# Attention's second tile divided ahead of normalising x, with two steps on the turned x moved back

## The reference

```python
h = _layernorm(x, axis=-1) * (1 + ca) + sa
x = x + ga * _L0_attn_ref(h, W_qkv, b_qkv, W_out, b_out)
h = _layernorm(x, axis=-1) * (1 + cb) + sb
x = x + gb * _L0_ffn_ref(h, w_gate, w_up, w_down)
```

```python
q = elu(q * E ** (-0.5)) + EPS_FEAT
k = elu(k) + EPS_FEAT
# for each token t in order
kv_s = kv_s + einsum('bhe,bhf->bhef', k_t, v_t)
k_s = k_s + k_t
out_t = einsum('bhe,bhef->bhf', q_t, kv_s) / (einsum('bhe,bhe->bh', q_t, k_s) + EPS_DEN)
```

## Time and the profile before

| What | Value |
|---|---|
| Time, median of 3 runs | 2003.87 us (2003.59 to 2005.35) |
| Profiled execution, its own time | 2005.31 us |
| Profiled execution, span of the core | 2003.5 us |
| PE busy | 1961.1 us (98% of the span) |
| DVE busy | 1439.8 us (72%) |
| ACT busy | 906.2 us (45%) |
| POOL busy | 873.5 us (44%) |
| TensorE clock granted, mean | 0.997 of full |

### The profile page before, as it was taken

One profiled execution on the slowest core, in us unless ns is written; L12 is line 12 of the kernel. 1 busy time (PEld: TensorE's weight loads), 2 busy tenths in 40 slices (PEclk: granted clock), 3 DMA queues, 4 the chain that ended last, 5 costly groups with the idle time before them and its releaser, 6 DMA issues. The chain is left out here.

```text
span 2003.5 us, 43850 instructions
## 1 busy us (share of the span) xinstructions
PE 1961.1 (98%) x16008; PEld 1592.4 (79%) x16008; DVE 1439.8 (72%) x2386; ACT 906.2 (45%) x1542; POOL 873.5 (44%) x718
## 2 busy tenths in 40 slices
PE   7999999999999999999899999999999999999999
PEld 4788888888888888887678888888888888888887
DVE  7977887877888877787875857658576585765744
ACT  5444444344444344444254536445364453644533
POOL 2533544444544444443334444444434444344444
PEclk9999999999999999999999999999999999999999
DMA  7223333444433434433475654656546565465553
GB/s 268 66 94 102 112 122 122 127 135 129 121 117 123 133 122 134 130 101 96 158 282 176 209 172 150 226 168 209 175 146 224 169 210 184 144 215 171 169 169 106
DMA packets 202521, 309.81 MB, mean 155 GB/s; under 512 B 16145, under 2 KB 72977, under 8 KB 202386
## 3 DMA queue, kind: packets, MB, share of 16 engines
q1 hardware_dynamic: 201858, 306.78, 48.0%
q10 hardware_dynamic: 528, 1.05, 0.1%
HBM read 225.19 MB, written 82.58 MB: 154 GB/s over the span
## 5 line engine op out<-in xcount | busy, mean ns | idle before, releaser
L1496 POOL TENSOR_TENSOR h_lo<-y_rows,h_hi 128x512 fp32r<-128x512 f32 x192 | 246.6, 1304 | 369.1 <-ACT h_hi L1594 369.0
L461 POOL TENSOR_TENSOR x_res<-y,x_res 128x512 f32<-128x512 f32 x64 | 82.9, 1296 | 293.9 <-DVE y L872 283.4
L851 DVE TENSOR_TENSOR probs<-sc,causal 128x512 f32<-128x512 f32 x256 | 158.3, 680 | 3.9 <-PE sc L1155 2.9
L612 ACT ACTIVATE z_exp<-pj,qk_neg 128x512 f32<-128x512 f32 x128 | 88.0, 687 | 161.5 <-PE pj L1136 159.1
L1136 PE MATMUL pj<-xt_hi,w_hi 128*128 128x512 f32 x512 | 146.3, 407 | 12.0 <-DVE a_t L861 10.8
L1924 PE MATMUL sc<-wd,h_hi 128*128 128x512 f32 x384 | 150.7, 392 | 0.0
L450 POOL TENSOR_TENSOR a_lo<-a_t,a_hi 128x512 fp32r<-128x512 f32 x60 | 82.4, 1373 | 154.5 <-ACT a_hi L626 154.5
L1924 PE MATMUL sc<-wd,h_lo 128*128 128x512 f32 x384 | 149.6, 390 | 0.0
L1136 PE MATMUL pj<-xt_lo,w_hi 128*128 128x512 f32 x512 | 138.8, 393 | 1.7 <-DVE xt_lo L789 1.7
L1136 PE MATMUL pj<-xt_hi,w_lo 128*128 128x512 f32 x512 | 138.2, 392 | 0.0
L1709 DVE TENSOR_TENSOR r_den<-pj,k_tok 128x512 f32<-128x512 f32 x96 | 66.2, 690 | 98.3 <-ACT k_tok L1577 52.6
(11 more groups left out here) (248 smaller groups left out, 5386.5 us busy)
## 6 DMA issues: line engine op xcount, KB each, us to landing
w_hi<-parts SPq DMA_DIRECT2D x48, 1024.0 KB, 5.4
w_lo<-parts SPq DMA_DIRECT2D x48, 1024.0 KB, 5.3
x_mid<-x_res SPq DMA_DIRECT2D x96, 256.0 KB, 2.9
x_res<-in_L_attn_x SPq DMA_DIRECT2D x64, 256.0 KB, 2.8
k_dram<-k_block SPq DMA_DIRECT2D x252, 64.0 KB, 1.8
xg<-in_L_attn_x SPq DMA_DIRECT2D x15, 1024.0 KB, 7.6
x_res<-x_mid SPq DMA_DIRECT2D x60, 256.0 KB, 4.0
full<-x_mid SPq DMA_DIRECT2D x60, 256.0 KB, 3.6
```

The costliest lines, as they stand in the source:

```text
L461: pool.tensor_tensor(out=x_res[:, slot, :], in0=y[:, :], in1=x_res[:, slot, :], op=ALU.add).then_inc(y_ready, 1)
L612: act.activation(z_exp[:, n % 2, :], pj[:, n % 2, :], ACT.Relu, bias=qk_neg[:, 1 - kind, c:c + 1], scale=-scale).then_inc(below_ready, 1)
L851: dve.tensor_tensor(out=probs[:, h, :].rearrange("p (c i) -> p c i", c=C), in0=sc[:, h, :].rearrange("p (c i) -> p c i", c=C), in1=causal[ ...
L1496: pool.tensor_tensor(out=h_lo[b], in0=h[i], in1=h_hi[b].bitcast(F32), op=ALU.subtract).then_inc(h_lo_ready, 1)
```

## The change

Three places, one on each of three engines. No instruction is added or removed.

- DVE, tile 1 of every group but the last: `divide` of tile 1 stands ahead of `norm_x(g + 2)` instead of behind it. Tile 2: `feature(n, other, 7)` stands ahead of `xt_low(g + 2, parity, 0)`.
- ACT: `exp_relu(n, 7)` stands ahead of `xt_full(g + 2, 0)` and `xt_high(g + 2, parity, 0)`.
- PE, tile 2: the first `x_turn` stands behind projection unit 7 (the eighth) instead of between units 6 and 7. Tile 3 is as before.

```diff
@@ scalar, ahead_of_last
             exp_relu(n, 5)
             exp_relu(n, 6)
+            exp_relu(n, 7)
             xt_full(g + 2, 0, x_bank)
             xt_high(g + 2, parity, 0)
-            exp_relu(n, 7)
             if looped:
                 act.wait_ge(down_out, g * 16 + (-16))
             xt_full(g + 2, 1, x_bank)
@@ vector, ahead_of_last
             feature(n, other, 4)
+            divide(g * GT + 1, g, parity, 1)
             norm_x(g + 2)
-            divide(g * GT + 1, g, parity, 1)
 
             mask(g * GT + 2)
...
             feature(n, other, 6)
+            feature(n, other, 7)
             xt_low(g + 2, parity, 0)
-            feature(n, other, 7)
             gate_last(g, 2)
@@ tensor, front
                 project(g + 1, 1 - parity, 3 * t)
-                if t >= 2:
+                if t == 3:
                     wait(pe, probs_ready, (g * GT + t) * HPC + 4)
                     x_turn(g + 2, 2 * t - 4, x_bank)
                 project(g + 1, 1 - parity, 3 * t + 1)
+                if t == 2:
+                    wait(pe, probs_ready, (g * GT + t) * HPC + 4)
+                    x_turn(g + 2, 2 * t - 4, x_bank)
```

## The result

The changed kernel takes 2008.52 us (median of 17 runs, 2006.3 to 2010.92) against 2004.86 (17 runs of the kernel before beside them): a ratio of 1.002, with a 95% interval of 1.0012 to 1.0027. That is 3.7 us more, a small loss of 0.2%. The stall that the change aims at is gone and a little more than its worth has come back elsewhere.

The account below looks back on a forecast made before the run. PE, busy 98% of the span, bounds the kernel. The removed stall is lost again to drawn-out norm_x: 12 groups at 0.2 us plus 3 at 0.1 give +2.7, a median of 2006.6 us; forecast's own range 2002 to 2009.

Parts of the forecast that it names:

- The wait on a_t: PE's projection matmul waiting for DVE's divided attention output: 10.8 us in 15 waits, 15.3 with restarts, all removed.
- The meeting: POOL's a_lo and next operation, pulled forward, meet DVE's third and fourth norm_x; the pair costs 1.92 us of DVE.
- gate_y: DVE, tile 2: ends at 469.83, so scores of tile 3 start later and a group loses 0.2 us.
- the second turn: PE, tile 2: waits 0.9 us for xt_full(0) and starts 0.2 earlier than before, not 1.17.
- The old collision of prod with DVE: POOL's prod against DVE's scan and xt_lo: replaced by feature 6 against prod, feature 6 ending 0.55 us after prod.
- Rival 1: DVE keeps the lock for the third norm_x, only the fourth is drawn out: -10.5 us, 1993.4; chance 0.17.
- Rival 2: No collision that matters, or one with slack behind it: the whole 15.3 us stall goes, 1988.6; chance 0.12.
- rival 3: Scores of tile 3 wait for gate_y in all 15 groups, 0.33 us each: +5.0, 2008.9; chance 0.17.
- a restart at the scores: PE, scores of tile 3: up to 0.14 us paid for resuming; rival 3 takes the full 0.14 in all 15 groups.
- the first turn: PE, tile 2, behind project 7: due at 462.9, said to wait 0.1 to 0.2 us for the masks (462.75).
- the turn costs PE the same at either place: PE, tile 2: moving the first x_turn behind project 7 leaves its cost on PE unchanged.
- The two rules of the Trainium skill: DVE and POOL: the lock rule gives the forecast's sum; the one-SBUF-input rule draws nothing out and gives 1988.6.

Follow-up runs that it names:

- the two runs of the changed order without a meeting: Changed kernel with add_bias and a_lo of each group's second tile cut to 4 columns: 1986.84 us; changed kernel with two norm_x ahead of den_of(n, 0): 1988.36 us.
- one meeting: Changed kernel with add_bias of the second tile of every group cut to 4 columns of 512, a_lo whole: 1992.26 us, ratio 0.9943.
- the control: Kernel before with add_bias and a_lo of the second tile of every group cut to 4 columns of 512: 2002.32 us, ratio 0.9994.

## Why the prediction was right

**What it got right, and the runs that show it.** The wait on a_t was worth about what was worked out: 15.3 us by the rows, 15.5 and 16.9 in the two runs of the changed order without a meeting. The meeting was where it was put, with its two prices: norm_x drawn out by 1.0 us twice (3.89 against 1.91), a_lo 0.08 ahead of the third. The runs with one meeting and with none took it away step by step, and the control shows that taking it away does nothing where nothing meets. That gate_y and not the second turn decides is shown by the run with exp_relu(7) where it was. The old collision of prod with DVE went as forecast: prod takes 1.29 us instead of 2.22 and xt_lo 0.69 instead of 1.50, and feature 6 takes 1.37 in its place. Rival 1 put one drawn-out norm_x at 1993.4, and the run with one meeting has 1992.26; but its reason, that DVE keeps the lock for the third norm_x, held in none of the groups. Rival 2 put no meeting at 1988.6, and the runs without one have 1986.84 and 1988.36.

**Where a size was off.** The forecast took 0.2 us a group and +2.7 in all; measured are 0.37 in the traces (59.87 - 59.50) and +3.7 in the medians. The forecast and rival 3 (0.33 a group, from 4.0 us in all) are one mechanism with two prices. The group's 0.37 lies beyond that of rival 3 and the 3.7 of the medians just short of its limit. But most of what rival 3 added was a restart at the scores (0.14), and there is none: the block behind them starts 1.10 us after them (470.89, 471.99), 1.11 before (469.77, 470.88).

Term by term: gate_y ends 14.09 us after the start of the first divide (470.15 + 0.68 - 456.74), where 13.96 were worked out (469.83 - 455.87). Of the 0.13, 0.07 stand in norm_x already (461.30 - 456.74 = 4.56 against 4.49), the rest in feature 7 and xt_low, which take up 0.61 and 0.60 where 0.57 each were taken. The scores of tile 3 start 14.15 after that divide, where the kernel before had 469.77 - 455.87 = 13.90: 0.25 of the 0.37 a group. The rest lies mostly in the other tiles, at 0.02 and in two of the eleven groups at 0.23 and 0.35; I did not settle what makes these. In all 15 groups together the traces have 4.6 us more. The two spans differ by 3.2, since the traced execution of the kernel before reached its first scores 1.3 us later (72.81 against 71.53), ahead of all that was changed.

Two steps came out otherwise, without weight in the sum. The prediction lets the first turn wait 0.1 to 0.2 us for masks that by its own figures (462.75) end before it is due (462.9), and it did not wait. The second turn starts 11.43 after the first divide, where 11.23 were worked out and the kernel before had 11.46, so it gained next to nothing; that is in the shadow of gate_y. That the turn costs PE the same at either place stood; the 0.13 us that the other moves cost alone are nearly all a wait of unit 7's weight load (0.12), which the early divide removes.

**The two rules of the Trainium skill.** SBUF — State Buffer, Who interferes with whom, has a tensor_scalar in its two-port mode take the port pair that VectorE and GpSimd share, for the whole of an instruction. The traces agree with that wait: 1.91 us for four norm_x alone, 2.89 with one meeting, 3.89 with two. Its other sentence, that one SBUF input outside that mode does not contend, holds here for the masks, which took 2.47 us beside a_lo and add_bias in the kernel before; norm_x is drawn out with one SBUF input, which by that page speaks for the two-port mode; no trace names the mode.

**By chance.** The forecast hung on 0.08 us between the starts of two instructions on two engines. In the changed kernel this distance is 0.08 to 0.09 us in all 15 groups, which is why it could be read at all. That the total came out near +2.7 is in part luck too: the groups cost nearly twice the 0.2 us that was taken for them.

## What to carry to other kernels

An instruction moved on a queue also moves what it releases. Follow the released work to where it will now run and see what it lies beside; here two POOL operations slid from the masks, which kept their pace beside them, to norm_x, which did not, and 2 us of drawn-out DVE work in each group took back the 15 us of removed waiting.
When an engine's busy time grows and its instructions do not, look for two engines whose operations draw each other out before you look at waits.
The longest wait in the list may stand in the shadow of a later one: ask which wait ends last, and move half of the work into idle time (here two of four norm_x) before you reorder all of it.

## What the runs showed of the hardware that was not expected

A wait of PE of some 2.5 us cost more than itself in 3 of the 15 groups of the run with the divide alone: the granted clock stood at 0.50 (1.2 GHz) for some 3 us, and the group was 1.3 us longer. Waits of the same length in the other groups left the clock at 1.00, and no wait of 1 us in the other runs did it.

A wait that holds up only a weight load leaves no idle time on the matmuls and still costs. Where it was 0.27 us, the block took 1.03 instead of 0.91, and the period was 0.13 longer (59.63 against 59.50). Where it was 0.33, the block also started 0.07 late, 0.19 in all, and in every other group, with 0.41, a little more. The period was 0.31 longer there (58.68 against 58.37) with PE busy throughout, and 0.06 of it lie in the other tiles, without a cause that was found. The waits are in the list of PEld, not of PE.
